# Fourteen scatters of a graph kernel issued one block later, and the scans that use their result moved behind the first gathers

## Chip, cores and metric

The kernel runs on one core of a Trainium2 chip. The metric is the device time of one execution in microseconds.

## What is computed

The input is 6250 nodes with 256 features and 100000 edges, already sorted by target. Two stages follow each other, each added to its own input:

```
x = x + gnn(layernorm(x), edges1)          # graph attention, 4 heads of 64
x = x + moe(layernorm(x), edges2)          # graph 2 has 131072 edges and the self loops
  h      = x @ W_gat                       # 16 numbers per node: 4 heads of 4
  e      = leaky_relu(a_src[src] + a_dst[dst])          # per edge and head
  alpha  = softmax of e over the edges of one dst
  scores = layernorm(sum(alpha * h[src]) + b_gat)       # mean over heads: 4 experts
  out    = sum over the 2 best experts of w * (gelu(x @ W1[e] + b1[e]) @ W2[e] + b2[e])
```

The change touches the second graph alone, and in it `a_dst[dst]`, which the kernel calls the own term of an edge.

## The kernel before, in words

The nodes lie in T = 49 tiles of 128, in seven batches of `BATCH` = 7. The program is a chain of blocks. In a block every engine runs its own list of instructions, and the next block starts when all engines have come to the end of theirs. The first two blocks do graph 1 and sort both lists of edges. The change is in the two blocks behind them.

**The middle block** turns the sums of graph 1 into nodes of the second stage. GpSimd brings the seven batches of sums (`col.bring`, line 969, an indirect DMA for each tile). VectorE, ScalarE and TensorE normalise a batch, project it, and write it to `rows2` (line 1382, which raises `mid.s_rows`). SyncE stores each batch to the tables in HBM (lines 1336 and 1337). GpSimd also scatters the own terms of each tile to where the run of edges of that node starts, in a tensor of HBM (`spread.set_starts`, line 557). It does so four batches behind the bringing: the variable `behind` in the block's GpSimd list. The last two batches of scatters wait for the last two batches of `mid.s_rows`.

**The second block** runs the experts on TensorE, ScalarE and VectorE, and at the same time the attention of graph 2. The attention works in units of 64 edges for each of the 128 partitions. GpSimd gathers the far rows of a unit, one indirect DMA for each column (`att.gpsimd`, line 618: 64 for unit 0, 48 for most later units; the 16 others are picked by TensorE, line 848, and VectorE, lines 878, 864 and 887). There are three buffers, `att.ring`. So the first three units are gathered in one go, and the gathers of a later unit wait until the unit three before it is stored. For each unit VectorE computes `att.scores` (lines 654 to 672), ScalarE the exponents (line 701), VectorE `att.weigh` (line 692 and others), and SyncE stores it (line 630). TensorE loops over seven rounds of the experts: `hidden` (line 1479), ScalarE's Gelu (line 1518), `product` (line 1493), VectorE's bias (line 1549), with picks between. VectorE's list is written out by hand: round 0 calls `hidden`, `hidden`, `products(0, 0)`, `hidden`, `products(0, 1)`, then `hidden` with `att.scores(v, 0)` inside it.

The own terms come back at the start of this block. SyncE waits for all 49 scatters and loads the whole tensor of 2 MB into `spread.seed` (`spread.sync`, line 570). `spread.first_rows` on GpSimd gathers the entry for the first column (line 563). `spread.vector` on VectorE then waits for both, copies that column in (line 577) and spreads the terms along the runs with four scans of 1024 columns, one for each head (line 580). `att.scores` of unit 0 is the first to read the result.

Of the kernel before, what the change touches and what calls it, by code (L numbers as in the profile page):

```python
# [28 lines left out]
BATCH = 7  # L29
# [2394 lines left out]
def gnn_moe_kernel(nc, x_dram, src, dst, W, a_l, a_r, W_gat, att_src, att_dst, b_gat, ln_gamma, ln_beta, W1, b1, W2,  # L2424
                   b2, edge_index, out_dram):
    N, DIM = x_dram.shape
    T = -(-N // P)
# [8 lines left out]
    with ExitStack() as ctx:  # L2436
        def sb(name, s, dt=F32, where=ctx):
            return where.enter_context(nc.sbuf_tensor(name, s, dt))
# [16 lines left out]
        with ExitStack() as stage:  # L2455
            order = Sort(nc, sems, q, stage, "e1", E1, src, dst, N, c, turned)
            np1 = First(nc, sems, q, stage, c, x_dram, W, a_l, a_r, own, table1, own_table1)
            with nc.Block() as block:
                @block.sync
                def _(sp):  # L2460
                    order.sync(sp)
                    np1.load(sp)
                    sp.wait_ge(s_far, 1)
                    for a in range(4):
                        sp.dma_start(starts1.rearrange("(a p j) h -> a p (j h)", a=4, p=P)[a], order2.buf[0][:, 0:800])\
                            .then_inc(s_low, 16)
                    np1.store(sp)
                    sp.wait_ge(s_low, 64)
                    sp.wait_ge(order.s_over, 1 + LONG)
                    sp.dma_start(flat.rearrange("(p j) -> p j", p=P), order.out[:, :]).then_inc(s_flat, 16)  # L2470
                    sp.wait_ge(s_flat, 16)
# [200 lines left out]
        with ExitStack() as second:  # L2672
# [3 lines left out]
            spread = Spread(nc, sems, q, second, "at2", runs, rows2[:, :, TW2:TW2 + HEADS], own_table2, TW2 + HEADS)  # L2676
            with ExitStack() as stage:
                acc1 = sb("acc1", [P, T, TW1 + HEADS], where=stage)
                col = Collect(nc, sems, q, stage, "co1", chains, att, acc1, c, xnT[:, 0, :])
                mid = Middle(nc, sems, q, stage, c, col, x_dram, x1, W_gat, att_dst, att_src, xnT, rows2, table2, own_table2)  # L2680
                with nc.Block() as block:
                    @block.sync
                    def _(sp):
                        mid.load(sp)
                        spread.clear_starts(sp)
                        mid.store(sp)

                    @block.gpsimd
                    def _(g):
                        col.fix(g)  # L2690
                        behind = 4
                        for b in range(mid.batches + behind):
                            if b < mid.batches:
                                for t in range(b * BATCH, (b + 1) * BATCH):
                                    col.bring(g, t)
                            if b >= behind:
                                g.wait_ge(mid.s_rows, b - behind + 1)
                                for t in range((b - behind) * BATCH, (b - behind + 1) * BATCH):
                                    spread.set_starts(g, t)

                    @block.vector
                    def _(v):
                        col.begin_vector(v)
                        mid.pad(v)
                        col.vector(v)
                        spread.clear(v)
                        mid.prepare(v)
                        mid.vector(v)

                    @block.scalar  # L2710
                    def _(a):
                        col.scalar(a)
                        mid.scalar(a)

                    @block.tensor
                    def _(pe):
                        col.tensor(pe)
                        mid.tensor(pe)
            with ExitStack() as stage:
# [23 lines left out]
                with nc.Block() as block:  # L2743
# [9 lines left out]

                    @block.gpsimd
                    def _(g):
                        spread.first_rows(g)
                        att.gpsimd(g)
                        col.bring_tails(g)
                        for t in range(T):
                            if t == 2 * BATCH:  # L2760
                                col.patch(g)
                            col.bring(g, t)
                        col.all_brought(g)

                    @block.vector
                    def _(v):
                        gates.begin(v)
                        pick.begin_vector(v, ffn.prod_space)
                        spread.vector(v)
                        att.begin_vector(v)  # L2770
                        ffn.begin_vector(v)
                        slots = iter(range(2 * pick.chunks))

                        def picked(many=1):
                            for _ in range(many):
                                pick.vector(v, att, next(slots))

                        def hidden(before=None, between=None):
                            if before:
                                before()  # L2780
                            picked()
                            if between:
                                between()
                            picked()

                        def products(r, e):
                            for half in range(2):
                                ffn.vector(v, r, e, half)
                                picked()

                        for r in range(ffn.rounds):
                            hidden((lambda: att.weigh(v, 2 * r - 2)) if r else None)
                            hidden(None, (lambda: att.scores(v, 2 * r - 1)) if r else None)
                            products(r, 0)
                            hidden(None, (lambda: att.weigh(v, 2 * r - 1)) if r else None)
                            products(r, 1)
                            hidden(None, lambda: att.scores(v, 2 * r))
                            products(r, 2)
                            products(r, 3)
                        last = att.units - 1  # L2800
                        att.weigh(v, last - 3)
                        att.scores(v, last - 2)
                        att.weigh(v, last - 2)
                        picked(2 * Pick.MORE // Pick.COLS)
                        att.scores(v, last - 1)
                        att.weigh(v, last - 1)
                        picked(2 * Pick.LAST // Pick.COLS)
                        pick.end_vector(v)
                        att.scores(v, last)
                        att.weigh(v, last)  # L2810
                        col.begin_vector(v)
                        col.vector(v)
                        gates.vector(v, 0)
                        v.sem_inc(mix.s_gates, 1)
                        gates.vector(v, 1)
                        v.sem_inc(mix.s_gates, 1)
                        for i in Mix.ORDER:
                            if i in Mix.BY_PE:
                                mix.add(v, i)
                            else:  # L2820
                                mix.weigh(v, i)
# [66 lines left out]
```

## Time and profile before

| what | value |
|---|---|
| three runs, us | 4067.5, 4070.69, 4030.13 |
| median, us | 4067.5 |
| the profiled execution, its own time, us | 4032.09 |
| its span from first to last instruction, us | 4030.4 |
| granted TensorE clock in it, mean | 0.713 |
| middle block in it, us from the start | 1896 to 2070 |
| second block in it, us from the start | 2070 to 4030 |

The profile is of one execution. Its times are read against 4032.09, and a difference worked out from it is then carried over to the median. POOL is GpSimd, DVE is VectorE, ACT is ScalarE, PE is TensorE, PEld its weight loads, SPq the DMA issues of SyncE.

### The profile page before, as it was taken

To read this page: it belongs to the slowest core of one execution; us is meant where nothing else is said; L and a number is where in the kernel's file an instruction comes from. 1 tells how busy PE (TensorE), PEld (TensorE's weight loads), DVE (VectorE), ACT (ScalarE), POOL (GpSimd) and SP (SyncE) were. 2 spreads that over 40 slices of the span, in tenths; PEclk is the share of its full clock that TensorE was granted. 3 is DMA by queue.
4 is the path that set the end of the run, shared out by engine and by line. 5 is a ranking of instruction groups with operands and counts; after the bars stand their busy time and mean duration, and the time that the engine had idled before them with its cause. 6 is when DMAs were issued, how large, how long until landed. Compare 5 with 4: busy or idle time off the path is not lost. (4 is left out here: it accounts for less than half of the span.)

```text
span 4030.4 us, 25984 instructions
## 1 busy us (share of the span) xinstructions
PE 1920.3 (48%) x7318; PEld 1431.0 (36%) x7322; DVE 1968.8 (49%) x3777; ACT 663.8 (16%) x1401; POOL 1745.5 (43%) x1787
## 2 busy tenths in 40 slices
PE   4415043444334354445541295554558475556425
PEld 3311032333223132324431274443446464444324
DVE  7875767555656554446520153333324343233646
ACT  6400011222112121112310011110101011011003
POOL 0015666555564444530767414344443424343241
PEclk9757566666667675767565697777779787777757
DMA  3211244544454343534521011111111111111415
GB/s 121 39 43 33 81 152 156 173 161 154 137 174 159 115 157 111 166 121 166 166 83 8 14 37 27 30 18 31 22 31 29 31 29 22 27 22 25 182 55 212
DMA packets 154183, 354.73 MB, mean 88 GB/s; under 512 B 55510, under 2 KB 96518, under 8 KB 144406
## 3 DMA queue, kind: packets, MB, share of 16 engines
q1 hardware_dynamic: 68303, 196.54, 13.5%
q0 software_dynamic: 69936, 121.07, 13.4%
q10 hardware_dynamic: 15866, 36.29, 2.3%
q8 instruction: 24, 0.39, 0.0%
q14 instruction: 54, 0.44, 0.0%
HBM read 181.01 MB, written 172.19 MB: 88 GB/s over the span
## 5 line engine op out<-in xcount | busy, mean ns | idle before, releaser
L618 POOL DMA_INDIRECT at_ring<-table,e_col x768 | 732.2, 953 | 1037.5 <-DMA at_sums<-at_ring 807.3
L2036 POOL DMA_INDIRECT at_ring<-table,at_idx x693 | 674.8, 974 | 561.8 <-DMA at_sums<-at_ring 358.8
L2128 PE MATMUL at_psS<-at_ring,at_hot 128*128 128x260 f32 x1584 | 484.9, 468 | 424.3 <-issue 271.7
L1493 PE MATMUL ffn_psY<-ffn_space 128*128 128x256 f32 x1568 | 393.8, 409 | 387.0 <-DVE ffn_space L1549 258.2
L1479 PE MATMUL ffn_psH<-xnT,ffn_space 128*128 x896 | 392.8, 590 | 333.0 <-ACT ffn_space L1518 195.8
L2128 PEld LDWEIGHTS at_psS<-at_ring,at_hot 128*128 128x128 f32 x1584 | 339.5, 231 | 560.4 <-issue 329.1
L878 DVE SCALAR_TENSOR_TENSOR pick_prod<-const_iota,pick_tile,pick_rows 128x400 f32<-128x400 f16 x256 | 158.5, 630 | 702.2 <-remote 392.8
L1493 PEld LDWEIGHTS ffn_psY<-ffn_space 128*128 128x128 f32 x1568 | 317.9, 206 | 449.0 <-DVE ffn_space L1549 271.5
L1479 PEld LDWEIGHTS ffn_psH<-xnT,ffn_space 128*128 128x128 f32 x896 | 271.6, 312 | 423.1 <-ACT ffn_space L1518 207.0
L2150 ACT ACTIVATE at_ring<-at_psS 128x520 f32<-128x520 f32 (+1 forms) x432 | 238.5, 567 | 745.9 <-PE at_psS L2128 377.4
L2229 DVE TENSOR_TENSOR at_ring<-at_ring,at_psW 128x1024 f32<-128x1024 f32 (+1 forms) x216 | 231.6, 1128 | 134.9 <-issue 96.8
L1518 ACT ACTIVATE ffn_space<-ffn_psH,ffn_b 128x448 f32<-128x448 f32 x224 | 141.4, 634 | 911.5 <-DMA at_sums<-at_ring 617.4
L1549 DVE TENSOR_TENSOR ffn_space<-ffn_psY,ffn_b 128x256 f32<-128x256 f32 x196 | 82.0, 424 | 425.5 <-DMA at_sums<-at_ring 265.8
L848 PE MATMUL pick_rows<-pick_table,pick_hot 128*128 128x400 f32 x1024 | 248.3, 388 | 75.5 <-issue 39.7
L848 PEld LDWEIGHTS pick_rows<-pick_table,pick_hot 128*128 128x128 f32 x1024 | 199.2, 205 | 94.8 <-issue 53.6
L2176 DVE TENSOR_TENSOR at_hot<-e_end_lane,at_psW 128x1408 f32<-128x1408 f16 (+1 forms) x72 | 115.6, 1617 | 203.2 <-PE at_psS L2128 143.8
L385 DVE TENSOR_SCALAR_CACHE_REDUCE rank_less<-turned,rank_node 128x400 bf16<-128x400 f32 (+1 forms) x196 | 129.5, 691 | 164.4 <-remote 114.5
L377 PE MATMUL turned<-rank_parts,rank_past 128*128 128x400 bf16 (+1 forms) x192 | 80.0, 417 | 133.8 <-DVE rank_less L385 88.1
L2023 POOL DMA_INDIRECT at_ring<-table,e_col x99 | 109.0, 1101 | 60.8 <-issue 29.6
L2116 PE MATMUL at_psW<-const_ident,at_both 33*128 33x33 f32 x192 | 23.8, 284 | 223.9 <-ACT at_both L2139 212.6
L887 DVE TENSOR_REDUCE at_ring<-pick_prod 128x32 f32<-128x800 f32 x128 | 125.7, 982 | 6.4 <-DMA at_sums<-at_ring 4.1
L969 POOL DMA_INDIRECT acc<-at_sums,e_end_idx x98 | 104.4, 1065 | 35.1 <-issue 29.2
(404 smaller groups left out, 2433.1 us busy)
## 6 DMA issues: line engine op xcount, KB each, us to landing
at_sums<-at_ring SPq DMA_DIRECT2D x72, 1452.0 KB, 4.9
products<-ffn_space ACTq DMA_DIRECT2D x28, 512.0 KB
at_ring<-table,e_col POOLq DMA_INDIRECT x867
at_sums<-at_ring SPq DMA_DIRECT2D x16, 768.0 KB, 3.2
late_space<-products SPq DMA_DIRECT2D x24, 512.0 KB, 7.3
at_ring<-table,at_idx POOLq DMA_INDIRECT x693
products<-ffn_space ACTq DMA_DIRECT2D x28, 384.0 KB
late_space<-products SPq DMA_DIRECT2D x24, 384.0 KB, 9.2
```

Of the source, the lines that this page charges most:

```text
L385: v.tensor_scalar(t.less[:, half, 0:H], self.ps[half], t.node[:, bass.ds(at + i, 1)], 0.0, ALU.is_lt, ALU.add, accum_out=t.n[:, bass.ds(at ...
L618: g.indirect_dma_start(self.ring[z][:, k, 0:TW], None, self.table, bass.IndirectOffsetOnAxis(ap=self.runs.col[:, u * U + k:u * U + k + 1], ...
L848: last = pe.matmul(self.ps_rows[n % self.BANKS][:, 0:S * D], self.hot[z][:, g, k * P:(k + 1) * P], self.table[:, part, g, :], start=(g == ...
L878: v.scalar_tensor_tensor(out=self.prod[:, k, :, :], in0=tiles, scalar=self.tile[:, n:n + 1], in1=self.ps_rows[n % self.BANKS][:, 0:S * D]. ...
L887: q.step(v.tensor_reduce(rows[:, at:at + 2, 0:D], self.prod[:, :, :, :], AX_X, ALU.add))
L1479: last = pe.matmul(self.psH[part][:, 0:half], self.w1[:, k, e * HID + f:(e + 1) * HID:FT], self.xnT[:, k, bass.ds(r * (BT * P) + part * ha ...
L1493: last = pe.matmul(self.psY[n % 2][:, 0:self.DIM], self.hid[:, e % 2, f, t * P:(t + 1) * P], self.w2[:, e * FT + f, :], start=(f == 0), st ...
L1518: a.activation(self.hid[:, e % 2, f, part * half:(part + 1) * half], self.psH[part][:, 0:half], ACT.Gelu, bias=self.b1[:, e * FT + f:e * F ...
L2036: g.indirect_dma_start(self.ring[z][:, k, 0:self.TW], None, self.table, bass.IndirectOffsetOnAxis(ap=self.idx[:, z, k:k + 1], axis=0)).the ...
L2128: last = pe.matmul(self.psS[at % 2][:, k - lo, 0:TW], self.hot[:, b, k, :], rows[:, b * self.SUB + k, 0:TW], start=True, stop=True)
L2150: a.activation(rows[:, b * self.SUB + lo:b * self.SUB + hi, 0:TW], self.psS[at % 2][:, 0:hi - lo, 0:TW], ACT.Copy).then_inc(self.s_out, 1)
L2229: q.step(v.tensor_tensor(part, part, self.weight[:, lo:hi, :].unsqueeze(3) .to_broadcast([P, hi - lo, HEADS, F]), ALU.mult))
```

## The change

The GpSimd list of the middle block leaves out the scatters of the last two batches, 14 tiles. The second block's GpSimd list begins with these 14 scatters, ahead of `first_rows` and of the gathers. On VectorE the call of `spread.vector` moves from the start of the second block to round 0, between `products(0, 1)` and the `hidden` that holds the scores of unit 0.

```diff
                         col.fix(g)
-                        behind = 4
+                        behind, later = 4, 2
                         for b in range(mid.batches + behind):
...
-                            if b >= behind:
+                            if behind <= b < mid.batches + behind - later:
                                 g.wait_ge(mid.s_rows, b - behind + 1)
                                 for t in range((b - behind) * BATCH, (b - behind + 1) * BATCH):
                                     spread.set_starts(g, t)
...
                     @block.gpsimd
                     def _(g):
+                        for t in range(T - 2 * BATCH, T):
+                            spread.set_starts(g, t)
                         spread.first_rows(g)
                         att.gpsimd(g)
...
                         pick.begin_vector(v, ffn.prod_space)
-                        spread.vector(v)
                         att.begin_vector(v)
...
                             products(r, 1)
+                            if r == 0:
+                                spread.vector(v)
                             hidden(None, lambda: att.scores(v, 2 * r))
```

## Rows read from the trace of the kernel before

**Rows 1.** The page: shares of the span, and the chain that ended last.

```profile
PE 1920.3 (48%) x7318; PEld 1431.0 (36%) x7322; DVE 1968.8 (49%) x3777; ACT 663.8 (16%) x1401; POOL 1745.5 (43%) x1787
...
PE 18%; another core or an unknown queue 16%; issue 7%; DVE 6%; POOL 1%; DMA 1%; ACT 0%; SPq 0%; ACTq 0%; POOLq 0%; DVEq 0%
```

**Rows 2.** Busy us (and instructions) of each stretch, then clock, DMA share, GB/s.

```profile
2062.00:2064.00 2.00, 0.00 (x0) 0.00 (x0) 0.00 (x0) 0.00 (x0) 0.00 (x0) 0.50 0.02 1
...
2395.00:2407.00 12.00, 12.00 (x44) 10.08 (x44) 3.86 (x5) 3.18 (x5) 8.96 (x10) 1.00 0.10 7
2407.00:2455.00 48.00, 13.56 (x35) 8.34 (x33) 7.50 (x16) 4.42 (x6) 36.41 (x39) 0.67 0.12 8
...
2465.00:2500.00 35.00, 31.98 (x127) 26.95 (x126) 22.42 (x48) 6.36 (x9) 0.00 (x0) 0.96 0.12 49
```

**Rows 3.** Timeline of POOL: start, duration, line, [idle time before and its releaser].

```profile
2060.54 0.98 POOL L557 DMA_INDIRECT at_starts<-rows,e_start_idx  x1 [0.30 <-issue]
2070.74 1.14 POOL L563 DMA_INDIRECT at_row<-own_table,e_row_idx  x1 [9.22 <-POOLq L2681]
2072.19 1.12 POOL L618 DMA_INDIRECT at_ring<-table,e_col  x1 [0.30 <-issue]
...
2092.77 2.30 POOL L618 DMA_INDIRECT at_ring<-table,e_col  x1 [0.30 <-issue]
2095.38 1.88 POOL L618 DMA_INDIRECT at_ring<-table,e_col  x1 [0.30 <-issue]
...
2275.76 0.95 POOL L618 DMA_INDIRECT at_ring<-table,e_col  x1 [0.30 <-issue]
2395.29 0.95 POOL L618 DMA_INDIRECT at_ring<-table,e_col  x1 [118.59 <-DMA at_sums<-at_ring]
```

**Rows 4.** Timeline of SyncE's DMA issues, at the start and end of blocks.

```profile
269.33 0.33 SPq L2470 DMA_DIRECT2D e_flat<-e_code  x1
272.34 0.33 SPq L1781 DMA_DIRECT2D at_ring<-e_flat  x1
...
2052.47 0.56 SPq L1337 DMA_DIRECT2D own_table<-rows  x1
2070.02 0.34 SPq L748 DMA_DIRECT2D own<-in_L_ffn_att_src  x1
```

**Rows 5.** Timeline of DVE and PE in the first gathers of the second block.

```profile
2091.82 0.17 DVE L577 COPY at_seed<-at_row 128x4 f32<-128x4 f32 x1 [12.19 <-issue]
2092.03 8.84 DVE L580 TENSOR_TENSOR_SCAN at_seed<-e_newrun,at_seed 128x1024 f32<-128x1024 bf16 x4
...
2085.32 8.10 PE L1479 MATMUL ffn_psH<-xnT,ffn_space 128*128 x16 [8.55 <-DMA ffn_space<-in_L_ffn_W]
2215.38 3.62 PE L1493 MATMUL ffn_psY<-ffn_space 128*128 128x256 f32 x8 [18.52 <-issue]
2237.78 3.78 PE L1493 MATMUL ffn_psY<-ffn_space 128*128 128x256 f32 x8 [17.05 <-issue]
```

**Rows 6.** Timeline of DVE and PE after the first gathers, around unit 0's scores.

```profile
2336.25 0.99 DVE L887 TENSOR_REDUCE at_ring<-pick_prod 128x32 f32<-128x800 f32 x1
2342.72 1.29 DVE L878 SCALAR_TENSOR_TENSOR pick_prod<-const_iota,pick_tile,pick_rows 128x400 f32<-128x400 f16 x2 [5.48 <-PE pick_rows L848]
2350.68 7.07 PE L1493 MATMUL ffn_psY<-ffn_space 128*128 128x256 f32 x32
2352.71 0.42 DVE L1549 TENSOR_TENSOR ffn_space<-ffn_psY,ffn_b 128x256 f32<-128x256 f32 x1
```

**Rows 7.** Line 557: duration in ns, min, median and max; and PE beside scatters alone.

```profile
L557 POOL DMA_INDIRECT at_starts<-rows,e_start_idx x49: 982/985/2091, 1970.0 to 2060.5; - x49
...
2026.10 0.98 POOL L557 DMA_INDIRECT at_starts<-rows,e_start_idx  x1 [0.30 <-issue]
2026.24 1.05 PE L1408 MATMUL mid_psH<-mid_w,xnT 128*128 128x24 f32 x4 [4.86 <-ACT xnT L1377]
```

**Rows 8.** The chain of waits, 2060 to 2120: start, us, what.

```profile
2112.56 2.10 another core or an unknown queue
```

## The prediction

> **What bounds the kernel now.** I read the page first. No engine is busy for even half of the span, and 16% of the last chain stands under "another core or an unknown queue" [rows 1]. So time is lost in waits, and the question is which ones the change touches. I then read the busy time by stretches. While GpSimd gathers, TensorE falls behind. In the second series of gathers TensorE runs fully for 12 us (12.00 busy of 12.00). Then, from 2407 to 2455, it is busy for 13.56 us of 48. Once GpSimd has been silent for 10 us it is busy for 31.98 us of 35 [rows 2]. The first series is the longest, 161 indirect DMAs from 2070.74 to 2276.71 [rows 3]. In it two tiles of products are 22.4 us apart (2215.38 and 2237.78), where each needs 16 records of matmul and weight load together, so some 1.4 us for each record [rows 5]. I can't say from the trace what holds TensorE. But the second block is, to a good approximation, series of GpSimd in which TensorE hardly moves, and full work of TensorE between them. GpSimd's next series starts at 2395.29, after 118.59 us of idle time [rows 3], once unit 0 is stored, and this hangs on the work that TensorE and VectorE do after the first series. A microsecond added to the first series, or to TensorE's work after it, therefore moves everything behind it. The same holds for the moment at which the second block starts.
>
> **Part 1: the middle block ends earlier.** The last scatter starts at 2060.54 and takes 0.98 us, so GpSimd has issued all at 2061.52 [rows 3]. The second block starts at 2070.02, with SyncE's first load [rows 4]. Nothing runs between: from 2062 to 2064 the DMA engines are 2% busy, and no engine executes anything [rows 2]. At another border of blocks, where GpSimd has long been idle, the last issue of SyncE at 269.33 is followed by the next block at 272.34, 3.0 us later, with the landing of its transfer included [rows 4]. So I take the 8.5 us after the last scatter as the price of closing GpSimd's list right after indirect DMAs, not as the price of the border. After the change GpSimd closes its list behind batch 4, long before the others (the 14 scatters left out are those that waited for ScalarE's last two batches). Last is then SyncE, with its table store issued from 2052.47 to 2053.03 [rows 4]. Adding 3.0 to 4.5 us for landing and border, the second block starts at 2056 to 2057.5; I take 2057, or **13 us earlier**. If the 8.5 us belong to every border of this kind, it starts 8.5 us after 2053.0 plus a landing of about 3, at 2064.5, and the gain is 5.5 us. That is the other end. ScalarE and TensorE of the middle block are not touched: in the code the last scatters wait for them (`mid.s_rows`), and nothing in that block waits for a scatter.
>
> **Part 2: the scatters at the head of the second block.** Fourteen scatters at 0.985 us (the median of line 557 [rows 7]) and 0.30 us between instructions [rows 3] are 14 x 1.285 = **18.0 us**, all ahead of `first_rows` and of the gathers. Their cover in the middle block is gone, since what they stand in front of is the series that stops TensorE. If each took the largest duration of line 557, 2.09 us, they would cost 33.5 us. That happens only beside a long vector instruction, and the vector instructions at the block's start are short, so I take the median. SyncE's load of the 2 MB now comes some 20 us after the block's start, where before it went out at about 6. The gathers don't need it and the scores of unit 0 come some 270 us later, so it costs nothing. The loads queued behind it on SyncE, of the gate's parameters, are needed after the experts: nothing too.
>
> **Part 3: the scans leave the first series.** VectorE's four scans ran from 2092.03 to 2100.87 [rows 5]. The gathers issued beside them took 2.30 and 3 x 1.88 us, against 0.95 for the others [rows 3] (two of the four and the last of the series stand there). That is 1.35 + 3 x 0.93 = 4.1 us by which the scans lengthened the series, and which it now loses: **-4.1 us**. (The Trainium skill, "SBUF — State Buffer", the part on the port pair that VectorE and GpSimd share, says that a vector instruction with two SBUF inputs and GpSimd exclude each other for a whole instruction. By that rule the four scans should each hold up one gather, and the trace agrees. By the same rule the scatters, which read SBUF, would be held up by the two-input instructions at the block's start.) I bound that last cost at 0 to 2 us, by the 0.17 us that the gather at 2072.19 took over 0.95, for some four scatters at one end, and one scatter at 2.09 instead of 0.985, twice, at the other; I take 0.5 us. TensorE gains nothing from the earlier free VectorE: it started on the experts at 2085.32, when the weights had landed [rows 5], and went on until the stall.
>
> **Part 4: the scans in front of unit 0's scores.** They now stand where TensorE is fully busy. VectorE ends line 887 at 2337.24 and is idle for 5.48 us, until TensorE's pick [rows 6]. Copy, wait and scans take 9.05 us (2091.82 to 2100.87 [rows 5]), so VectorE is free at about 2346.6 instead of 2342.72, 3.9 us late. Everything to the first bias of the next product follows back to back, so it comes at 2356.6 instead of 2352.71. TensorE can run two tiles of products ahead (eight matmul records each, 7.07 us for four tiles, so 3.5 us from 2350.68 [rows 6]), and wants the first bias done at 2354.2; it gets it at 2357.0. That makes **+2.8 us**, between 0 (if the stall has left TensorE late anyway) and 9.1 (if nothing covers the scans).
>
> **Part 5: what TensorE does in the longer series.** From the block's start to the end of the series it takes 18.0 - 4.1 + 0.5 = 14.4 us more. At some 1.4 us for a record TensorE does ten records in that, and ten records are about 1 us of full work: **-1 us**.
>
> **Sum.** -13 + 18.0 + 0.5 - 4.1 + 2.8 - 1 = +3.2 us. On the profiled execution this is 4032.1 + 3.2 = 4035.3 us. The three timed runs lie on two levels 1% apart (4030 and 4068 to 4071), and the profiled one is on the lower; I carry the same +3 us to the median, 4067.5 + 3 = **4070.5 us**. What a measurement of this kernel can tell from no change is about 1%, 40 us, so this is no change. With the terms at their ends the sum goes from -13 + 18.0 + 0 - 4.1 + 0 - 1 = -0.1 to -5.5 + 18.0 + 2 - 4.1 + 9.1 - 0 = +19.5.
>
> **Rivals.**
> Faster: TensorE's stall is tied to the gathers, not to scatters. In the first series it ran from 2085.32 until the chain first shows unknown waits at 2112.56, 42 us after the block's start [rows 5, 8]. If that end moves with the first gather, which is now 20 us behind the block's start and not 2, TensorE works fully for 18 us more, and the sum is 3 - 18 = -15 us, 4052.5. For it speaks that the onset came only 12 us after the start of the second series [rows 2], so it isn't a fixed time, and something in the first series puts it off. Against it speaks the middle block, where between 2018 and 2037 GpSimd did nothing but scatters and TensorE's four-matmul steps still had 4.86 us of idle time between them [rows 7] (one scatter of that stretch stands there).
> Slower: the block doesn't start earlier and the scatters are slow. If something else than GpSimd closes the middle block at 2070, the 13 us are lost (+16), and if the loads of the weights or VectorE slow the scatters at the block's head to 2.09 us, that is 15.5 us more, +31.7 us in all, 4099. It decides from the point where the border stays within 5 us of 2070; it is +0.8%, so even then short of 1%, and passes it only if the scans lie wholly on TensorE's path too (9.1 for 2.8: +38) and something small is added. The silence before 2070 speaks against it.
> Nothing happens: the second block absorbs head and scans, since a later series just meets TensorE elsewhere. That is 4067.5 +- 5, and can't be told from my sum.
> The levels: the median of the changed kernel's runs may fall on the lower level, near 4033, whatever the change does. I can't exclude it, since two of four executions seen are there.
>
> **How the numbers follow.** My sum has a chance of 0.5, absorbed 0.15, the faster rival 0.2, the slower one 0.15. Within 1% lie the first three, and most of the fourth. Leaving room for levels that pair badly, I give 0.06 faster, 0.87 within 1%, 0.07 slower. The range goes from the lower level less a few us (4025) to the upper level with the sum's upper end (4070.7 + 19 = 4090).
>
> **What would show it.** First: the second block's first load at 2056 to 2058, with GpSimd idle for some 20 us before it. Second: 14 rows of line 557 in its first 19 us, then line 563, then gathers, none of them at 1.88 us. Third: the last gather of the first series at 2057 + 0.7 + 18.5 + 1.4 + 200.4 = 2278.0 (first instruction, scatters, line 563, and the old gathers' 2072.19 to 2276.71 less 4.1), within 2 us of the old 2276.7. Fourth: line 577 at about 2337, a late first line 1549 behind the scores, and unit 3's first gather 2 to 4 us later than 2395.29. My prediction is wrong if TensorE's stall ends at another distance from the last gather, or if the border stays at 2070.

## The result, and the profile after

The changed kernel took 4069.8 us (median of 20 runs, 4053.9 to 4107.5), and the kernel before 4052.0 us beside it (20 runs, 4029.2 to 4070.7). The ratio is 1.0046, with a 95% interval from 1.0027 to 1.0066, so it is about 18 us slower. That is inside the 1% which counts as no change here, and 0.7 us from the predicted 4070.5. The agreement with the number is luck: the sum gave +3 where the medians differ by +18, and the kernel before came out 15.5 us below the 4067.5 that the sum was added to. The 20 runs of before fill the whole stretch from 4029 to 4071. So there are no two levels of time, as I had read into three runs.

One thing has to be known before the numbers of the experiments can be read. The chips differ. On some, among them those of the recorded pair, TensorE comes nearly to a stop while GpSimd issues its series of gathers (here: **holding chips**, 4012 to 4052 us for the kernel before). On others it doesn't (**free chips**, 2779 to 2780 us for the same kernel). Every ratio below is between kernels on one chip. Where counts of instructions or single times are set beside those of another chip, it is said. That the difference goes with the chip rests on the four chips of the experiments, two of each kind; the one that came up twice was free both times.

The profiled execution of the changed kernel took 4070.6 us with a span of 4068.9, against 4032.1 and 4030.4. Of these 38.5 us, 16.2 lie before the middle block even starts (1896.20 and 1912.37), in stages that the change doesn't touch. The middle block is 12.4 us shorter (161.4 for 173.8) and the second block 34.8 us longer (1995.2 for 1960.4). Only these last two belong to the change: +22 us, close to the +18 of the medians.

The page first, with the rows that answer to [rows 1]:

```profile
PE 1934.8 (48%) x7318; PEld 1435.4 (35%) x7322; DVE 1968.6 (48%) x3777; ACT 665.1 (16%) x1401; POOL 1739.8 (43%) x1787
...
PE 17%; another core or an unknown queue 14%; issue 11%; DVE 6%; POOL 0%; DMA 0%; ACT 0%; ACTq 0%; SPq 0%; DVEq 0%; POOLq 0%
```

The busy times are those of before to within a per cent. Work has not changed, only its place. Next the stretches of the changed kernel, with busy us and instructions of PE, PEld, DVE, ACT and POOL, then clock, DMA share and GB/s. They answer to [rows 2]:

```profile
2071.00:2073.00 2.00, 0.00 (x0) 0.00 (x0) 0.00 (x0) 0.00 (x0) 0.00 (x0) 0.50 0.00 0
...
2073.75:2133.75 60.00, 16.87 (x48) 10.32 (x48) 9.61 (x31) 5.00 (x7) 45.24 (x48) 0.61 0.39 121
2133.75:2273.75 140.00, 31.56 (x52) 14.23 (x52) 5.72 (x8) 5.08 (x8) 105.85 (x113) 0.56 0.11 8
...
2430.00:2442.00 12.00, 12.00 (x45) 10.11 (x44) 3.84 (x5) 3.18 (x5) 9.05 (x10) 1.00 0.09 8
2442.00:2490.00 48.00, 13.36 (x35) 8.17 (x33) 6.83 (x15) 4.42 (x6) 36.41 (x39) 0.65 0.10 8
```

The last two are the second series of gathers, and they are a copy of [rows 2]: 12 us of full work, then 13.4 us of 48. The two before them are the first series, and this is where the new loss sits: TensorE starts 48 matmuls in the first 60 us of the block and 52 in the next 140. Before the change it was 109 and 69, in the same stretches from that block's start:

```profile
2070.02:2130.02 60.00, 38.02 (x109) 25.91 (x110) 26.86 (x50) 11.23 (x17) 46.16 (x44) 0.78 0.39 122
2130.02:2270.02 140.00, 21.26 (x69) 15.92 (x67) 3.95 (x7) 3.15 (x4) 105.85 (x113) 0.57 0.13 12
```

The timeline shows the change itself. POOL and SP answer to [rows 3] and [rows 4], and DVE and PE to [rows 5] and [rows 6]:

```profile
2059.20 0.98 POOL L557 DMA_INDIRECT at_starts<-rows,e_start_idx  x1 [0.30 <-issue]
2074.18 0.98 POOL L557 DMA_INDIRECT at_starts<-rows,e_start_idx  x1 [13.99 <-POOLq L2681]
...
2090.95 0.99 POOL L557 DMA_INDIRECT at_starts<-rows,e_start_idx  x1 [0.30 <-issue]
2092.25 1.04 POOL L563 DMA_INDIRECT at_row<-own_table,e_row_idx  x1 [0.30 <-issue]
2093.59 0.99 POOL L618 DMA_INDIRECT at_ring<-table,e_col  x1 [0.30 <-issue]
...
2292.45 0.94 POOL L618 DMA_INDIRECT at_ring<-table,e_col  x1 [0.30 <-issue]
2430.21 0.95 POOL L618 DMA_INDIRECT at_ring<-table,e_col  x1 [136.82 <-DMA at_sums<-at_ring]
...
2069.23 0.56 SPq L1337 DMA_DIRECT2D own_table<-rows  x1
2073.75 0.34 SPq L748 DMA_DIRECT2D own<-in_L_ffn_att_src  x1
...
2369.58 0.17 DVE L577 COPY at_seed<-at_row 128x4 f32<-128x4 f32 x1
2369.79 8.84 DVE L580 TENSOR_TENSOR_SCAN at_seed<-e_newrun,at_seed 128x1024 f32<-128x1024 bf16 x4
...
2088.71 7.72 PE L1479 MATMUL ffn_psH<-xnT,ffn_space 128*128 x16 [8.33 <-DMA ffn_space<-in_L_ffn_W]
...
2105.43 3.37 PE L1479 MATMUL ffn_psH<-xnT,ffn_space 128*128 x4 [5.71 <-ACT ffn_space L1518]
2149.52 3.38 PE L1479 MATMUL ffn_psH<-xnT,ffn_space 128*128 x4 [40.73 <-issue]
...
2388.95 3.72 PE L1493 MATMUL ffn_psY<-ffn_space 128*128 128x256 f32 x16 [2.34 <-DVE ffn_space L1549]
```

Read them from the top. GpSimd's last scatter of the middle block ends at 2060.2, SyncE's last store goes out at 2069.23, and the second block begins at 2073.75. The head scatters follow each other every 1.29 us, and none takes more than 1.00 us. TensorE gets its weights 15 us into the block, as before, works densely for some 11 us, and then stands still from 2108.8 to 2149.5 with no releaser but "issue". The series ends at 2293.4, which is 219.6 us after the block's start, where it was 206.7. After it GpSimd waits 136.82 us for unit 0's store, where it had waited 118.59 [rows 3]. So the second block loses 13.0 us in a longer series and 18.2 us in the work that was still left when the series ended.

The releaser "issue" hides who is late in that gap. The other engines' rows show it:

```profile
2096.46 1.70 PE L848 MATMUL pick_rows<-pick_table,pick_hot 128*128 128x400 f32 x8
2126.52 0.63 DVE L878 SCALAR_TENSOR_TENSOR pick_prod<-const_iota,pick_tile,pick_rows 128x400 f32<-128x400 f16 x1 [42.48 <-remote]
2137.64 0.63 DVE L878 SCALAR_TENSOR_TENSOR pick_prod<-const_iota,pick_tile,pick_rows 128x400 f32<-128x400 f16 x1 [10.48 <-remote]
2148.84 0.63 ACT L1518 ACTIVATE ffn_space<-ffn_psH,ffn_b 128x448 f32<-128x448 f32 x1 [43.47 <-DMA at_sums<-at_ring]
2160.04 0.63 ACT L1518 ACTIVATE ffn_space<-ffn_psH,ffn_b 128x448 f32<-128x448 f32 x1 [10.57 <-DMA at_sums<-at_ring]
```

TensorE's two picks (line 848) end at 2098.16. VectorE's line 878, which waits for a pick, starts on the first of them 28 us later. ScalarE's Gelu starts at 2148.84, 40 us after the matmuls of 2105.43 have ended, and TensorE's next step, which waits for a Gelu, follows it by 0.7 us. So TensorE isn't slow at its matmuls: what comes late is the signal that they are done, and then all three engines wait in a circle. The trace also holds the times at which semaphores were raised, and they say the same: TensorE's for the two picks at 2126.41 and 2137.61, and for the matmuls of 2105.43 at 2148.81. In the run without head scatters, told of below, eleven signals of TensorE from 2103.83 to 2238.23 come 11.2 us apart, with one step of 33.6. The few signals of ScalarE's Gelu that were recorded in these gaps come within 0.02 us of its end. "TensorE's stop" below means this state.

### The profile page after: what moved, and what is told of

Same layout as the page of the kernel before. It is cut to its first block and busy times, and to the rows that moved or that the text cites. A ratio compares the mean times of both kernels' runs of the same rounds, so it can differ in the third digit from the quotient of the medians.

```text
span 4068.9 us, 25984 instructions
## 1 busy us (share of the span) xinstructions
PE 1934.8 (48%) x7318; PEld 1435.4 (35%) x7322; DVE 1968.6 (48%) x3777; ACT 665.1 (16%) x1401; POOL 1739.8 (43%) x1787
## 3 DMA queue, kind: packets, MB, share of 16 engines
q1 hardware_dynamic: 68303, 196.54, 13.4%
## 5 line engine op out<-in xcount | busy, mean ns | idle before, releaser
L2128 PE MATMUL at_psS<-at_ring,at_hot 128*128 128x260 f32 x1584 | 492.8, 474 | 426.6 <-issue 295.8
L1479 PE MATMUL ffn_psH<-xnT,ffn_space 128*128 x896 | 406.9, 606 | 512.2 <-ACT ffn_space L1518 260.3
L1493 PE MATMUL ffn_psY<-ffn_space 128*128 128x256 f32 x1568 | 382.3, 400 | 235.5 <-DVE ffn_space L1549 224.5
```

Of the source, the lines that this page charges most:

```text
L1479: last = pe.matmul(self.psH[part][:, 0:half], self.w1[:, k, e * HID + f:(e + 1) * HID:FT], self.xnT[:, k, bass.ds(r * (BT * P) + part * ha ...
L1493: last = pe.matmul(self.psY[n % 2][:, 0:self.DIM], self.hid[:, e % 2, f, t * P:(t + 1) * P], self.w2[:, e * FT + f, :], start=(f == 0), st ...
L2128: last = pe.matmul(self.psS[at % 2][:, k - lo, 0:TW], self.hot[:, b, k, :], rows[:, b * self.SUB + k, 0:TW], start=True, stop=True)
```

## The experiments

Two theories stood after the result, and both explain the early stop of TensorE. **A, the lost brake:** the four scans used to slow the gathers beside them to 2.2 us from one to the next, TensorE worked meanwhile, and the change took that away. **B, the scatters:** the head scatters stop TensorE as gathers do, so its stop comes 18 us earlier.

### The halves of the change

Scatters at the head, scans at their old place:

```diff
                         pick.begin_vector(v, ffn.prod_space)
+                        spread.vector(v)
                         att.begin_vector(v)
...
-                            if r == 0:
-                                spread.vector(v)
```

> The 14 scatters stand at the head of the second block as in the changed kernel, but the scans (lines 577 and 580) stay at the start of the second block. Theory A (the scans beside the first gathers slowed the gathers from a pitch of 1.25 to 2.2 us for 9 us, and TensorE lived on that: its stall begins 42 us after the start of the block with them, 25 us without): TensorE's stall begins some 15 us later than in the changed kernel and the second block is shorter by 10 us or more than the changed kernel's 1995 us. Theory B (the scatters themselves starve TensorE earlier, 14 more indirect DMAs ahead): the stall begins as early as in the changed kernel, about 25 us after the block's start, and the second block takes 1995 us +- 5.

Scans moved, scatters in the middle block as before:

```diff
-                        behind, later = 4, 2
+                        behind = 4
...
-                            if behind <= b < mid.batches + behind - later:
+                            if b >= behind:
...
-                        for t in range(T - 2 * BATCH, T):
-                            spread.set_starts(g, t)
```

> The scans alone move in front of unit 0's scores; all scatters stay in the middle block. Theory A: TensorE's stall begins near 25 us after the start of the second block, not 42; the first series is 4 us shorter, the scans cost 2.8 us on TensorE's path, and the sum is 10 to 15 us slower than before (ratio 1.003). Theory B: the stall begins at 42 us as before, and the sum is -4.1 + 2.8 = about -1 us, ratio 1.000.

These and the next two ran on a free chip (before: 2779.0 us). Scatters only: 2769.6 us, ratio 0.9965 [0.9953, 0.9978]. Scans only: 2781.1 us, 1.0010 [1.0002, 1.0019]. The border shows in both: the middle block takes 148.9 us with the scatters gone from it and 168.2 with them, so on that chip it is worth 19 us. The other expectations hang on a TensorE that stops, and are tested in neither run. The scans alone gain nothing. Left at their old place behind late scatters they seem to cost: VectorE waits 18.05 us for the seed there, and the second block takes 1172.6 us instead of 1164.8 in the full change on another free chip (next section).

### A brake put back, and the scatters left out

Four scans that nobody reads, beside the first gathers of the changed kernel:

```diff
                         pick.begin_vector(v, ffn.prod_space)
+                        v.wait_ge(spread.s_row0, 16)
+                        for _ in range(HEADS):
+                            q.step(v.tensor_tensor_scan(ffn.prod_space[:, 0:spread.J], spread.runs.newrun[:, :],
+                                                        ffn.prod_space[:, 0:spread.J], -BIG, ALU.add, ALU.max))
+                            q.wait()
                         att.begin_vector(v)
```

> The changed kernel with four more scans of 1024 columns on an unused space, right after the first column of own terms has landed, so beside the first gathers where the real scans once were. Theory A: the four gathers beside them take 1.9 to 2.3 us, the first series is 4 us longer than in the changed kernel, but TensorE's stall begins 10 us or more later and the whole is 5 to 12 us faster than the changed kernel. Theory B: 4 us slower than the changed kernel, since it only lengthens the series.

The kernel before without its last 14 scatters, so that the own terms of tiles 35 to 48 are left out of the result:

> The kernel before without the last 14 scatters at all (the own terms of tiles 35 to 48 are left out); scans at their old place. If closing GpSimd's list right after indirect DMAs cost 8.5 us and the scatters held the border, the middle block takes 161 us and not 174, the second block 1960 us as before, and the whole is 13 us faster, ratio 0.9968. If the border is bound by something else, the middle block keeps 168 us or more.

Brake: 2768.7 us, 0.9966 [0.9953, 0.9980]. No late scatters: 2759.2 us, 0.9924 [0.9911, 0.9937]. The last one prices the border: its middle block takes 148.4 us where it takes 168.2 with these scatters, so on this chip they hold the border by 20 us, more than the 13 expected. The other three I had written with a TensorE in mind that stops. On this chip it doesn't, so they could not tell A from B. The changed kernel itself ran next, on another free chip:

> The changed kernel itself, beside the kernel before, to see whether this chip shows TensorE's long stalls in GpSimd's series (4052 and 4070 us) or not (2779 us in the runs so far). With the stalls: ratio 1.0046 again, 18 us slower, second block some 35 us longer. Without them: from the two halves taken alone (scatters 0.9965, scans 1.001) the sum is -9.5 + 2 = 7.5 us faster, ratio 0.997; a theory by which the scatters' 18 us stand wholly in front of the second block expects slower than before by some 5 us instead.

It took 2765.0 us against 2779.7, ratio 0.9940 [0.9926, 0.9953]: **14.7 us faster** (7.5 were expected), where the same kernel is 18 us slower on the holding chip of the recorded pair. The windows show why (second block, first 60 and next 140 us), and the rows of SyncE and GpSimd show the border:

```profile
1599.31:1659.31 60.00, 47.25 (x174) 37.59 (x175) 25.50 (x57) 14.49 (x21) 45.04 (x47) 0.83 0.42 129
1659.31:1799.31 140.00, 137.64 (x563) 117.54 (x562) 88.02 (x156) 30.45 (x43) 107.21 (x108) 0.99 0.21 43
```

```profile
1585.33 0.56 SPq L1337 DMA_DIRECT2D own_table<-rows  x1
1590.97 0.98 POOL L557 DMA_INDIRECT at_starts<-rows,e_start_idx  x1 [0.30 <-issue]
1599.31 0.34 SPq L748 DMA_DIRECT2D own<-in_L_ffn_att_src  x1
```

POOL is about as busy as on the holding chip (47 and 108 instructions for 48 and 113), but TensorE starts 563 matmuls in the 140 us in which it started 52. With TensorE running through the series, the brake gives nothing and only costs: the ratio is 0.9966 with it and 0.9940 without, and the second block takes 1166.4 and 1164.8 us (two free chips). The head scatters hardly show in the second block: 1164.8 us with them and 1164.4 in the run of the scans alone, on the other free chip. The earlier border remains. What closes the middle block here is still GpSimd: its last scatter ends at 1591.95, after SyncE's last store, and the next block follows 7.4 us later. It is 7.4 us too in the three runs of the other free chip whose last 14 scatters were gone from that block, and 8.5 in the scans-only run, where all 49 stand in it. On the holding chip GpSimd ends 9 us ahead of SyncE's last store, and SyncE closes.

### On a holding chip: which theory

For a control, the kernel before on a holding chip:

> The kernel before, unchanged, for its trace on this chip. If TensorE's stalls are absent here (near 2779 us), the middle block ends with GpSimd's scatters some 30 us after SyncE's last store, and TensorE is busy all through the gathers of the second block. If they are present (near 4052 us), the trace looks like the one of before.

It took 4007.8 us, with 113 and 65 matmuls in the two stretches, as in the first trace. Beside it ran the changed kernel without its 14 head scatters (the own terms of tiles 35 to 48 are left out of the result):

```diff
-                        for t in range(T - 2 * BATCH, T):
-                            spread.set_starts(g, t)
                         spread.first_rows(g)
...
-        sp.wait_ge(self.s_set, 16 * self.runs.T)
+        sp.wait_ge(self.s_set, 16 * (self.runs.T - 2 * BATCH))
```

> The changed kernel without the 14 scatters at the head of the second block (the own terms of tiles 35 to 48 are left out). It prices the head. Without stalls on this chip: TensorE, not GpSimd, bounds the second block and hides most of the 18 us, so this is 2 to 8 us faster than the changed kernel (2765 us); if GpSimd's series bounds the block, it is 18 us faster. With the stalls: theory A (lost brake) expects 13 to 18 us faster than the changed kernel's 4070 us and a stall that still begins 25 us after the block's start; theory B (the scatters starve TensorE) expects 30 us or more and a stall that begins later.

It took 4006.0 us, 0.9979 [0.9959, 0.9999]. The two stretches, and TensorE's gap:

```profile
2036.60:2096.60 60.00, 15.67 (x48) 10.30 (x48) 12.14 (x33) 5.00 (x7) 45.23 (x48) 0.61 0.40 122
2096.60:2236.60 140.00, 32.01 (x52) 14.84 (x52) 2.88 (x4) 5.08 (x8) 105.95 (x112) 0.56 0.13 8
```

```profile
2104.54 3.38 PE L1479 MATMUL ffn_psH<-xnT,ffn_space 128*128 x4 [38.73 <-issue]
```

48 and 52 matmuls, the very counts of the changed kernel, with no scatter at the head, and the stop begins 29 us into the block (at 2065.8). **B falls: the scatters don't bring the stop forward.** What is missing in both kernels is the scans beside the first gathers. The total does not decide it. From 1.0046 to 0.9979 are 0.67%, some 27 us, where A had 13 to 18 and B 30 or more, and the two intervals together leave room for 11 to 43. The run also prices the head scatters: unit 0's store is issued 334.9 us after the block's start and not 353.0 (two holding chips), so they cost 18.1 us, as the sum had them.

The same brake as above was then run on a holding chip:

> Changed kernel plus four scans that nobody reads, as long as the own-term scans (one SBUF result, newrun and one fp32 SBUF source), started on VectorE when the row of first terms has landed, so beside the first gathers of the second block. They copy the brake of the kernel before to its old place. Where TensorE has the long stalls beside GpSimd's series (the kernel before above 3900 us): by the theory of the lost brake the gathers beside the scans take 1.9 to 2.3 us each, TensorE's stall starts at least 10 us later than 25 to 29 us into the block, 60 or more matmuls stand by +60 us instead of 48, and the time is 5 to 13 us below that of the changed kernel, ratio 0.999 to 1.002 to the kernel before. By the rival (the head scatters starve TensorE) the stall starts at 25 to 29 us as in the changed kernel and the ratio stays at 1.0046. Where the long stalls are absent (the kernel before near 2779 us), both give 0.9935 to 0.997.

It took 4051.6 us against 4041.5, 1.0021 [0.9994, 1.0047], just above the 0.999 to 1.002 of theory A. The interval overlaps that of the changed kernel (1.0027 to 1.0066, another chip), so the total leaves it open; the trace doesn't:

```profile
2076.40:2136.40 60.00, 36.89 (x109) 25.78 (x109) 27.15 (x45) 11.34 (x17) 46.49 (x44) 0.78 0.38 120
2136.40:2276.40 140.00, 24.64 (x69) 18.40 (x68) 3.95 (x7) 3.15 (x4) 105.87 (x113) 0.56 0.11 12
```

```profile
2097.49 2.79 POOL L618 DMA_INDIRECT at_ring<-table,e_col  x1 [0.30 <-issue]
2100.59 2.03 POOL L618 DMA_INDIRECT at_ring<-table,e_col  x1 [0.30 <-issue]
...
2420.64 0.94 POOL L618 DMA_INDIRECT at_ring<-table,e_col  x1 [119.69 <-DMA at_sums<-at_ring]
```

109 and 69 matmuls, to the piece what the kernel before had. Four slow gathers (2.79 us and three of 2.02 to 2.03) lengthen the series by 5 us, and GpSimd's wait for unit 0 falls from 136.82 to 119.69. So the brake costs 5 us and gives 17: unit 0's store is issued 340.8 us after the block's start and not 353.0. Scans whose result nobody reads bring back 12 us of the second block: theory A. While they run, TensorE's signals still come at most 2.8 us apart; in the changed kernel the first one that is late, at 2104.72, comes 9.8 us after the one before. The rule of the Trainium skill ("SBUF — State Buffer", in the part on the two sides) that the prediction drew on, that a VectorE instruction with two SBUF inputs and a GpSimd instruction that reads SBUF exclude each other, agrees with these four gathers. It does not show at the block's head, where all 14 scatters took 0.98 to 1.00 us beside short instructions. Beside an addition of 2.02 us in the middle block (line 1367) a scatter of the changed kernel took 2.42.

### Is it the pitch of the gathers?

The pitch is the time from the start of one gather to the start of the next. First each gather waited for the landing of the one before:

```diff
             for k in range(U - self.picked[u]):
+                if k:
+                    g.wait_ge(self.s_rows[z], landed + 16 * k)
                 g.indirect_dma_start(self.ring[z][:, k, 0:TW], None, self.table,
```

> The changed kernel with each gather of the second block issued only when the one before it has landed, so that GpSimd's pitch is about 2.3 us instead of 1.25. On a chip with the stalls this is the direct test of theory A: if a pitch of 2.2 us is what let TensorE go on beside the scans, TensorE runs beside the whole series and the kernel is far faster than 4070 us, some 3700 us or less; theory B, or any by which TensorE's stall is tied to the gathers whatever their pitch, expects it slower by some 700 us (730 gathers by 1 us). On a chip without stalls GpSimd becomes the bound: 730 gathers by 1 us more than the 919 us series, so slower by some 500 us.

It took 4323.3 us, 1.0772 [1.0733, 1.0811], which neither theory had (at most 3700 by A, 700 more than before by B). Two stretches, and a gather between the first and last of them:

```profile
2056.00:2147.00 91.00, 91.00 (x364) 77.72 (x364) 47.79 (x66) 23.50 (x34) 31.75 (x31) 1.00 0.16 45
2147.00:2242.00 95.00, 0.85 (x5) 0.43 (x4) 6.72 (x16) 0.60 (x1) 34.25 (x37) 0.53 0.06 4
```

```profile
2083.40 0.94 POOL L621 DMA_INDIRECT at_ring<-table,e_col  x1 [1.69 <-DMA at_ring<-table,e_col]
```

Most gathers come 2.65 us after the one before, 31 of them in the first stretch (2.9 us on the mean), and TensorE is busy for all of 91 us: it isn't held. Then it runs out of work, since the scores wait for rows that now come too slowly, and GpSimd is the bound. The pace was too slow, but the mechanism showed. So the next kernel kept the gathers free of waits on their landing and only spread them, with two memsets of 128x192 on a tile of its own before each:

```diff
             for k in range(U - self.picked[u]):
+                for _ in range(2):
+                    g.wait_ge(self.s_idle, self.idles)
+                    g.memset(self.idle[:, :], 0.0).then_inc(self.s_idle, 1)
+                    self.idles += 1
                 g.indirect_dma_start(self.ring[z][:, k, 0:TW], None, self.table,
```

> Changed kernel with two memsets of 128x192 by GpSimd (each waited for by the next) ahead of each of the attention stage's gathers, so a pitch of about 1.8 to 2.0 us between gathers instead of 1.25, without waiting for any transfer. Where the long stalls are present: by the theory that TensorE is starved by the pitch of the gathers, it works through the series, the first series lasts 290 to 320 us with over 200 matmuls by +200 us instead of 100, and the second block is bound by 729 gathers x 1.9 = 1385 us and what follows: kernel 3450 to 3750 us. By the theory that the stall comes from the transfers being unwaited for, whatever their pitch (the waits on landings of the paced run ended it), the stalls stay and the kernel takes 4300 to 4700 us. Where the long stalls are absent: the second block grows from 1165 us to some 1500 us, kernel 3050 to 3200 us.

On the chip of the brake's second run (before: 4041.5 us) it took **3587.3 us, ratio 0.8848 [0.8805, 0.8890]**. Its stretches, its two groups on POOL (busy, mean ns, then idle before them), and the chain that ended last:

```profile
2080.72:2140.72 60.00, 44.67 (x161) 35.06 (x162) 22.74 (x51) 14.50 (x21) 50.18 (x87) 0.84 0.37 121
2140.72:2280.72 140.00, 116.72 (x472) 99.55 (x472) 74.94 (x127) 26.05 (x37) 122.69 (x243) 0.91 0.16 38
```

```profile
POOL 33%; issue 6%; DVE 2%; DMA 1%; PE 0%; ACT 0%; SPq 0%; POOLq 0%; DVEq 0%
...
L623 POOL DMA_INDIRECT at_ring<-table,e_col x768 | 738.9, 962 | 128.4 <-issue 126.4 <-POOL at_idle L621 2.0
L621 POOL MEMSET at_idle<- 128x192 f32 x1536 | 411.5, 268 | 44.3
```

GpSimd executes 1536 instructions of no use more, and the kernel is 454 us faster, within the 3450 to 3750 us of the theory that the pitch starves TensorE, and far from the 4300 to 4700 of its rival. The pitch is (738.9 + 128.4 + 411.5 + 44.3) / 768 = 1.72 us instead of 1.25. TensorE starts 472 matmuls in the 140 us instead of 52, and "another core or an unknown queue" is gone from the chain. The memsets also make GpSimd wait for each of them, and this run alone doesn't separate that from the pitch; the scans of the brake widened the pitch without such a wait. The same kernel and one with a single memset were then run together, on a free chip (before: 2779.9 us):

> Changed kernel with one memset of 128x192 ahead of each gather instead of two: pitch about 1.49 us (0.96 gather + 0.27 memset + 0.26 issue), first and later series together 768 x 1.49 = 1144 us instead of 768 x 1.73 = 1329. Where the long stalls are present: if TensorE gets through at this pitch, GpSimd stays the bound and the kernel takes 3587 - 180 = about 3400 us; if it is starved in part (the theory that the stall grows as the pitch falls below some 1.7 us), 3600 to 3950 us; if wholly, 4000 or more. Where the long stalls are absent: the second block is bound by 1144 us and its ends, kernel 2850 to 2950 us.

> The kernel with two fillers beside the one with one, on the same chip, for the difference of the two. Where the long stalls are present: about 3587 us again, ratio 0.88 to 0.89. Where they are absent: GpSimd's 768 x 1.73 = 1329 us bind the second block, kernel 2765 + (1500 - 1165) = about 3100 us, so that the same edit loses 12 per cent there.

One memset: 2858.9 us, 1.0284 [1.0267, 1.0302]. Two: 3099.8 us, 1.1152 [1.1134, 1.1171]. Both lie where the sum for a chip without the stop had put them. The stretches of the second:

```profile
1595.50:1655.50 60.00, 47.82 (x176) 37.96 (x176) 25.94 (x58) 14.49 (x21) 49.90 (x87) 0.83 0.39 128
1655.50:1795.50 140.00, 113.44 (x456) 96.69 (x455) 71.62 (x123) 25.76 (x37) 122.62 (x243) 0.90 0.15 35
```

Beside the holding chip's rows above they are nearly equal, and so are the whole second blocks: 1502.3 us on the holding chip (3583.0 - 2080.7) and 1503.5 on the free one (3099.0 - 1595.5). At a pitch of 1.72 us nothing of the difference between the chips is left in this block. The 484 us by which the two executions still differ lie before it. Whether 1.49 us is wide enough on a holding chip wasn't tried. No kernel here beats both on both kinds of chip: the changed one is best where TensorE runs freely, and the spread gathers where it doesn't.

## Why the prediction was right, and which step of it was not

**Part 1, the border: right.** 13 us were forecast, and the middle block is 12.4 us shorter. What closes it is SyncE's store: the next block starts 4.0 us after its issue has ended (2069.79), within the 3.0 to 4.5 that were allowed. The start came at 2073.75 and not at 2057, because this execution was 16.2 us late before it.

**Part 2, the head scatters: right.** 18.0 us and 0.5 for contention were forecast. The first scatter to line 563 is 2092.25 - 2074.18 = 18.1 us, so contention was next to nothing, and leaving them out moves unit 0's store by 18.1. The load of the seed, issued at block + 19.4, delayed nothing.

**Part 3, the first half: right.** No gather takes 1.88 or 2.30 us any more; the series ends 13.0 us later in the block, where 18.0 + 0.5 - 4.1 = 14.4 was forecast.

**Part 3, the second half, and part 5: wrong, and the largest error.** "TensorE gains nothing from the earlier free VectorE", and "-1 us" for ten records more. I had counted what the scans take from GpSimd, and not what slower gathers give to TensorE. The kernel before did 109 matmuls in the first 60 us, since four gathers in 9 us let it work on. With these gathers at full pitch it did 48. 200 us into the block 78 matmuls more were left over (100 against 178 started), and GpSimd's wait for unit 0 grew by 18.2 us: the 2.3 of the scans on TensorE's path and **15.9 where the sum had -1**. The run without head scatters gives the same term, with nothing of them in it: 334.9 - 321.5 (the store of unit 0 in the two traces of before, mean) + 4.1 - 2.3 = 15.2 us. The run with the brake gives 17. The prediction's fourth sign says it too: line 577 came 295.8 us after the block's start, where 2337 - 2057 = 280 was forecast. And the 1.4 us for a record, by which part 5 got its -1, was no rate of TensorE: in [rows 5] a tile's matmuls take 3.6 to 3.8 us and 17 to 18.5 us of waiting stand before them, 22.4 us from tile to tile, twice the 11.2 us of TensorE's late signals.

**Part 4, the scans before the scores: right.** +2.8 was forecast. TensorE waits 2.34 us for line 1549 behind them.

With the missed term the sum up to unit 3's first gather is -12.4 + 13.0 + 15.9 + 2.3 = +18.8 us, and the medians say +18. In the two profiles 3.6 us more fall behind that gather (34.8 - 31.2), and no run explains these. **The faster rival** (the stop is tied to the gathers and would come later) had seen that something in the first series puts the stop off, and looked for it at the block's start. It was the scans. Had I asked it of them, its sign would have turned round: the change removes what puts the stop off. **The slower rival** had the right sign by a wrong cause: the border moved and no scatter of the head was slow. **Absorbed**: not so, since the series and all behind it moved by 31 us at unit 3's first gather (356.5 us after the block's start for 325.3). The 20 runs of before show no two levels.

The range held, because 1% of this kernel is 40 us and no term of the change is that large. It would not have held the free chips' 2765 us, which nothing in the trace of one chip could show.

## What to carry to other kernels

When two engines are said to slow each other, ask who else lives on the slow one's pauses. Here four scans that held up GpSimd's gathers looked like a cost of 4 us, and moving them away cost some 15 us, since TensorE had worked in those pauses. An idle engine without a releaser may be waiting for another one that heard too late of its own work, so look when each engine's consumers start. Where TensorE's idle time has no releaser and falls together with a long series of indirect DMAs, vary the pitch of the series before anything else is reordered. And run such a kernel on more than one chip before tuning by tens of microseconds: the same edit was worth -15 us on one and +18 on another.

## What the runs showed of the hardware

**The stop of TensorE is a matter of chip and pitch.** On holding chips TensorE is nearly stopped beside a series of GpSimd's gathers of 128 short rows at a pitch of 1.25 us. Its matmuls are not what is late, but the signals that they are done: 11.2 us from one to the next in the run without head scatters, where they come every 1.5 to 1.7 us within a round of matmuls on a free chip. The lower clock (0.56) doesn't explain the steps: four matmuls take 3.38 us at it, and 1.72 at 2097.99. The stop sets in 12 us after the second series' start; in the first it begins 27 us after the first gather without head scatters, and with them 15 us after the first gather (2093.59 to 2108.8) but 35 after the first scatter. TensorE then starts 52 matmuls in 140 us. At 2.65 us it is not held, and at 1.72 us it starts 472. On free chips it starts 563 at a pitch of 1.25. What holds the signals back stays open. It isn't the bytes: in TensorE's gap the changed kernel's DMA engines are a tenth busy, and one queue alone moves anything. These are the rows of the DMA view from 2108.8 to 2149.5:

```profile
DMA packets 1056, 0.34 MB, mean 8 GB/s; under 512 B 528, under 2 KB 1056, under 8 KB 1056
...
q0 software_dynamic: 1056, 0.34, 9.9%
```

No packet of the two instruction queues falls in that gap either.

**GpSimd's list closes late after indirect DMAs.** From the last scatter's end to the next block are 8.5 us in the three traces in which all 49 scatters stand in the middle block, and 7.4 us in the six free-chip traces with 35 there. Where GpSimd ended 9 us ahead of SyncE's last store, as on the holding chip after the change, this time cost nothing.

**Small instructions on GpSimd can speed up a kernel**, as long as they stand between indirect DMAs and GpSimd isn't the bound: 1536 memsets of 0.27 us gave 454 us there, and cost 335 us on a free chip (3099.8 against the changed kernel's 2765.0, the same chip in another job).
